# Matmuls on a zeroed tile ahead of the first product of a graph attention kernel

## What is computed

```
h = relu(layernorm(x));  x = x + smooth(h, adj)
h = relu(layernorm(x));  x = x + attention_and_mlp(h, adj, weights)

smooth:    B = (adj + adj.T) / 2 + I;  deg = sum(B, axis=1);  dinv = deg ** -0.5
           y = (adj @ (dinv[:, None] * B * dinv[None, :])) @ h
attention: 8 heads of 64, softmax over the neighbours, then four dense layers
```

## Time and profile before

| | |
|---|---|
| median of 3 runs | 863.55 us |
| all runs | 863.52, 863.55, 865.99 us |
| profiled execution: its own time | 865.98 us |
| its span (first to last instruction) | 864.2 us |
| TensorE matmul busy | 841.9 us, 97% |
| VectorE, ScalarE, GpSimd busy | 703.5, 427.9, 281.0 us |
| DMA | 87.97 MB, mean 102 GB/s |

### The profile page before, as it was taken

One profiled execution on the slowest core, in us unless ns is written; L12 is line 12 of the kernel. 1 busy time (PEld: TensorE's weight loads), 2 busy tenths in 40 slices (PEclk: granted clock), 3 DMA queues, 4 the chain that ended last, 5 costly groups with the idle time before them and its releaser, 6 DMA issues.

```text
span 864.2 us, 15276 instructions
## 1 busy us (share of the span) xinstructions
PE 841.9 (97%) x5207; PEld 757.4 (88%) x5207; DVE 703.5 (81%) x1224; ACT 427.9 (50%) x793; POOL 281.0 (33%) x299
## 2 busy tenths in 40 slices
PE   2999999999999999999999999999999999999998
PEld 2888888888888888887899999999999999999886
DVE  6899886557656885587999999999999999998864
ACT  3445333321111111256766666666666666785753
POOL 0000000000000000066875555555566644556322
PEclk9999999999999999999999999999999999999999
DMA  9979831703222222051340000000001022000144
GB/s 345 406 273 372 354 97 59 209 0 121 97 97 98 97 97 73 1 195 27 112 142 17 22 26 26 26 24 24 26 26 25 21 87 76 26 2 2 49 147 148
DMA packets 37627, 87.97 MB, mean 102 GB/s; under 512 B 7168, under 2 KB 8320, under 8 KB 37568
## 3 DMA queue, kind: packets, MB, share of 16 engines
q1 hardware_dynamic: 35504, 82.98, 27.7%
q10 hardware_dynamic: 2064, 4.26, 1.3%
HBM read 74.45 MB, written 12.78 MB: 101 GB/s over the span
## 4 chain that ended last, share of the span: by engine, by line
PE 92%; DMA 3%; DVE 3%; ACT 2%; issue 1%; POOL 0%; ACTq 0%
PE bank L1835 27%; PE bank L77 14%; PE bank L79 14%; PE bank L78 14%; PE bank L1879 14%; PE bank L554 3%; DMA l_src<-e_rows 1%; DMA e_rows<-rows 1%; PE bank L2413 1%; PE bank L2407 1%; PE bank L2352 1%; PE bank L2409 1%; DMA l_h<-x 1%; PE bank L1010 0%; DVE e L915 0%
## 5 line engine op out<-in xcount | busy, mean ns | idle before, releaser
L1359 DVE SCALAR_TENSOR_TENSOR l_q<-bank,neg_d,mask 128x512 fp32r<-128x512 f32 x512 | 339.0, 740 | 23.5 <-PE bank L1835 23.5
L1835 PE MATMUL bank<-l_parts,l_q 128*128 128x260 f32 x2048 | 250.5, 283 | 1.6 <-ACT l_o_m L1533 1.6
L1835 PEld LDWEIGHTS bank<-l_parts,l_q 128*128 128x128 f32 x2048 | 246.9, 188 | 2.6 <-ACT l_o_m L1533 1.9
L77 PE MATMUL bank<-x_hi,s_hi 128*128 128x512 f32 x448 | 174.5, 389 | 0.0
L79 PE MATMUL bank<-x_hi,s_lo 128*128 128x512 f32 x448 | 174.3, 389 | 0.0
L78 PE MATMUL bank<-x_lo,s_hi 128*128 128x512 f32 x448 | 174.3, 389 | 0.0
L784 POOL TENSOR_TENSOR l_prod<-wh,l_a 128x512 f32<-128x512 f32 x29 | 34.1, 1195 | 382.5 <-ACT wh L745 380.2
L1526 ACT ACTIVATE l_o_q<-bank 128x260 f32<-128x260 f32 x128 | 49.0, 388 | 104.7 <-PE bank L1835 97.5
L79 PEld LDWEIGHTS bank<-x_hi,s_lo 128*128 128x128 f32 x448 | 84.1, 188 | 17.6
L78 PEld LDWEIGHTS bank<-x_lo,s_hi 128*128 128x128 f32 x448 | 84.1, 188 | 17.3
L77 PEld LDWEIGHTS bank<-x_hi,s_hi 128*128 128x128 f32 x448 | 84.1, 188 | 17.3
(11 more groups left out here) (229 smaller groups left out, 1191.0 us busy)
## 6 DMA issues: line engine op xcount, KB each, us to landing
rows<-adj_t SPq DMA_DIRECT2D x48, 512.0 KB, 3.8
l_now<-adj SPq DMA_DIRECT2D x16, 512.0 KB, 7.0
l_rows_k<-adj_t SPq DMA_DIRECT2D x16, 512.0 KB, 7.9
l_src<-e_rows SPq DMA_DIRECT2D x32, 256.0 KB, 3.2
l_kept<-adj SPq DMA_DIRECT2D x12, 512.0 KB, 13.2
wh_store<-wh ACTq DMA_DIRECT2D x1, 4160.0 KB, 14.6
l_h<-x SPq DMA_DIRECT2D x4, 1024.0 KB, 17.2
x<-x SPq DMA_DIRECT2D x1, 4096.0 KB, 13.4
```

The costliest lines, as they stand in the source:

```text
L77: pe.matmul(acc, hi, rhs_hi, start=first, stop=False, skip_group_check=True)
L1359: v.scalar_tensor_tensor(out=q[:, i, :], in0=bank[S_BANKS[hh]][:], scalar=neg_d[:, i, h:h + 1], in1=mask[:, i, cols], op0=ALU.is_ge, op1=A ...
L1835: return pe.matmul(bank[Q_BANKS[hh][t]][:, 0:PW], q[:, i, t * P:(t + 1) * P], parts[pair_slot][:, i, hh * PW:(hh + 1) * PW], start=i == 0, ...
```

## The change

A third instruction on GpSimd zeroes the last 512 columns of `early_lo`, the place of the feature rests of step 3. TensorE waits for it and then multiplies that tile by itself: 36 matmuls of 128x128 by 128x512 into bank 7, then a wait for the first head of B (`hi_ready` 1), then 7 more. The results are dropped, since step 0 starts bank 7 anew. Everything behind it is as before.

```diff
@@ smooth_features
     def gpsimd(p):
         p.memset(ident[:], 0.0).then_inc(ident_made, 1)
         p.wait_ge(ident_made, 1)
         p.affine_select(out=ident[:], in_=ident[:], compare_op=ALU.not_equal, fill=1.0, base=0,
                         pattern=[[-1, P]], channel_multiplier=1).then_inc(ident_made, 1)
+        p.memset(early_lo[:, EARLY - 1, :].bitcast(F32), 0.0).then_inc(ident_made, 1)
     def tensor(pe):
+        def keep_busy(count):
+            for _ in range(count):
+                pe.matmul(bank[G8 - 1][:], early_lo[:, EARLY - 1, 0:P], early_lo[:, EARLY - 1, :], start=True, stop=True)
         pe.sem_inc(slot_free, 2)
+        pe.wait_ge(ident_made, 3)
+        keep_busy(36)
+        pe.wait_ge(hi_ready, 1)
+        keep_busy(7)
         def products(s, b, early=None, first=False, last=False, bank_free=None):
```

## The result

The changed kernel takes 867.27 us at the median of 14 runs (865.31 to 868.88), the kernel before 864.00 (863.1 to 865.99, 14 runs). The ratio is 1.0032, with a 95% interval of 1.0024 to 1.0040: 3.3 us slower by the medians, 2.8 (2.1 to 3.5) by the ratio, where 0.4 us less was forecast.

A forecast was written before the change was run, and what follows sets the result against it. TensorE, busy 97% of the span, was taken as the bound. Memset 0, filler 0, step 0 -2.98 and new idle time +2.58 sum to -0.40 us: 863.15 us from the median 863.55, range 861.8 to 865.7.

The forecast's parts named there:

- step 0: First 24 matmuls, from 15.50 us: at the upper clock they end at 20.94 instead of 23.92, 2.98 us earlier.
- steps 1 to 3: Following steps at the start: each waits for its feature head, cutting the gain to 1.99, 1.77 and 1.55 us.
- the chunk of x: Second chunk of x, landing near 41.5 us: decides when step 5 starts; nothing in the change makes it land sooner.
- step 5: Waits for the rest of B from `cut_lo(5)`: starts at 45.28 instead of 45.68, leaving only 0.40 us of gain.
- Past it the program is the same: Everything after the start: TensorE's waits are small and triggered loads start 0.40 us earlier too, so the gain persists.
- the filler at 0: Added matmuls from about 2.3 to 15.0 us, wholly in the 15.5 us wait before step 0: no cost.
- the row at 441.89: Wait of 1.65 us late in the kernel; matmuls behind it keep 0.120 us, so such a gap costs nothing.
- Rival 2: Slow stretch at the start is shorter in timed runs than profiled: no gain, 863.55; chance 0.22 together with another rival.
- Rival 4: Filler at the start runs late and delays step 0, so the kernel is slower: 866.5 us; chance 0.06.

The follow-up runs named there:

- g1: Kernel before plus 41 matmuls in a never-taken branch at the filler's place, no filler run: 866.75 us against 864.06, ratio 1.0025.
- e2: Changed kernel with the filler as two hardware loops of two 512-column matmuls per body: 864.50 us, ratio 1.0003 to the kernel before.
- e1: Changed kernel with the same 43 filler matmuls, of 16 columns instead of 512: 867.85 us, ratio 1.0041 to the kernel before.
- f4: Looped filler of e2 with the second chunk of x loaded ahead of tile 5: 863.38 us, ratio 0.9993 to the kernel before.
- g2: f4 run once more: 864.98 us, ratio 0.9998 to the kernel before.
- e3: Changed kernel with 128 filler matmuls of 16 columns instead of 43 of 512: 878.08 us against 863.97 for the kernel before.
- f2: Changed kernel with 26 + 7 filler matmuls and 92 more ahead in a never-taken branch: 864.84 us, ratio 1.0009 to the kernel before.
- f1: Changed kernel with 85 small matmuls added in the never-taken retry branch near the program's end: 866.12 us, ratio 1.0018 to the kernel before.
- f3: Kernel before with the second chunk of x loaded ahead of tile 5, no filler: 864.09 us against 864.15.
- e0: Kernel before, rerun unchanged: 865.02 us, with 863.97 for the same kernel beside it.

## Why the prediction was wrong

**What held.** The filler lay wholly in the wait (its last start is about 14.5) and raised the clock; step 0 lost nothing; VectorE and ScalarE held steps 1 to 3; the chunk of x held step 5. Of step 0's 2.98 us, 0.52 was left at step 5 (45.68 - 45.16), against 0.40. That this agrees so well is in part luck: beside the other four profiles without a raised clock (45.16 to 45.45), the changed kernel's 45.16 is 0 to 0.3 us sooner. On average the kernels with the filler and the old order of loads start step 5 at 45.04 (45.16, 45.01, 44.93, 45.05), the five without at 45.36. So some 0.3 us is the better figure for what the start gives.

**Where it failed.** The step is *"Past it the program is the same"*, and the sum in front of it, which had the filler at 0 because it ran in idle time. The filler's time was free, but its code was not: 43 matmuls with their weight loads are 86 instructions more in TensorE's stream, and everything behind them lies elsewhere in the 16 KB pieces in which that stream is fetched. A program with those instructions and without the filler's work (g1) is slower by 2.7 us, and one with the work and 16 instructions (e2) is not slower by anything that can be told. I never priced an instruction as an instruction. Two terms are missing:

- *The end, +1.6 us.* The over goes from 1.8 to 3.4. It does so with 86 instructions moved (changed, e1, g1), not with 16 (e2, f4, g2), nor with about 256 (e3, f2), and padding behind the middle of the program alone takes it back (f1). The closing events come 2.0 to 2.3 us after the last instruction in the three, 0.2 to 0.3 in all others. That the place of the code does this is shown. How it does so is not: the last fetch on record starts 0.0 to 0.5 us before the end of the span and ends 0.4 to 0.9 us behind it in all kernels alike, with the loss and without, and none is recorded after that. That the closing instructions lie beyond a border of a piece in the three, and so wait for it, is the reading that fits; the addresses themselves are not in the trace.
- *The store of scores, 5.55 to 6.71 us.* Its length has two values only: 5.53 to 5.62 in eight profiles and 6.71 to 6.73 in four, and the four are those whose code is moved by 86 in the middle. In these four a fetch of queue 8 starts 4.7 us after the store and lasts 0.9 us (between 432.2 and 434.0), and the store's last semaphore write follows 0.2 us behind the end of that fetch. In the eight others no fetch starts until 2.1 us or more after the store is complete. The packet is late by 0.6 us; the rest of the 1.16 us lies between its record and the end of the wait (0.9 us in the four, 0.3 in the others), and what fills it is not on record. In the profiles TensorE waits for the same chain anyway (1.65 us in the earlier trace rows), which hides some of it. In the timed runs the spans of g1 are 0.9 us longer at the median than before's beside them (863.2 against 862.3); as the end and this together make g1's 2.7 us, the difference gives 1.1.

**What is left.** 867.27 is 0.5 over g1, although the filler should have brought some 0.3 less, and e2, f2, f4 and g2, free of both losses, are not faster than before by what their starts gained. The start's gain is not lost early: in every profile TensorE's lead or lag against the kernel before is the same to 0.05 us at 395 us as at 60. What changes it comes behind 400 us. One part shows in the records. At the wait near 441 us the clock sometimes falls to its lower level. In e2's profile the wait is

```profile
439.94 7.31 PE L1845 MATMUL bank<-l_parts,l_q 128*128 128x260 f32 x45 [1.43 <-ACT l_o_m L1543]
```

and the stretches behind it (us, TensorE busy (x), granted clock, DMA share, GB/s) are

```profile
438.00:441.40 3.40, 1.96 (x13) 1.00 0.34 98
441.40:444.80 3.40, 3.40 (x18) 0.50 0.10 35
444.80:448.00 3.20, 3.20 (x29) 1.00 0.00 0
```

18 matmuls in 3.4 us where about 28 fit: the same 126 matmuls take 17.01 us here and 15.47 in the profile before, 1.5 us more. The prediction used the row at 441.89 to say that such a gap costs nothing; it costs nothing in some executions only. The profiles of f3 and g2 have the fall too, behind waits of 1.43 and 1.97 us, and those of the kernel before and e0 have none behind 1.65 and 1.71, so the length of the wait does not decide it.

The mean granted clock of each run tells how often it falls. Runs at 0.999 are hardly longer than those at 1.000; those at 0.998 or less have spans some 1.8 us longer (863.95 against 862.13 in the 81 runs of the kernel before). They are 30 of 70 in the kernels with a raised clock at the start and 31 of the 128 others, which makes 0.3 us on average. That is not the whole rest: among the runs at 0.999 or 1.000 alone, the mean span is 862.7 in e2 (9 runs) and 862.6 in f2 (5 runs), still 0.5 *over* the 862.1 of the kernel before. But e0, which is the kernel before itself, has 862.6 as well (9 runs), so half a microsecond between two sets of runs can be chance.

With the chunk of x ahead, the same mean is 861.5 (12 runs of f4 and g2), 0.6 under the kernel before, and at the lower values 863.3 against 863.95, again 0.6 under. So the two edits together may gain 0.6 us, which the more frequent fall (11 of 23 runs against 17 of 81) hides in the totals; sorted so after the fact, and with e0's scatter beside it, this is a hint and no proof. Why an early start should make the fall more frequent, and whether anything else costs e2 and f2 their gain, stays open.

**The rivals.** None was this one. Rival 2 came true in part: the slow stretch at the start of step 0 differs from run to run (the clock rises 4.5 to 6.1 us after the first matmul of the product in the six profiles where nothing had raised it), and the profile in hand had the longest. That takes away some of the gain and cannot make the kernel slower. Rival 4 had the sign and, by chance, nearly the size (866.5), but its mechanism, a late filler, did not occur. The range ended at 865.7, near the highest run of the kernel before, because every case in it took TensorE's start as the only thing that the change touched.

## What to carry to other kernels

Work put in idle time is free only if its code is: count the instructions that it adds, and where a 16 KB fetch then falls, at the program's end and beside the small DMAs that others wait for. Put filler in a hardware loop, where 44 matmuls cost 16 instructions here, and compare with a kernel that has the same instructions in a branch never taken; that tells code from work in one run. Compare a run's own time with its span before looking for a loss in the trace, since it may lie behind the last row.

## What the runs showed that I had not expected

- TensorE's stream is fetched through queue 8 in pieces of 16 KB that take 0.9 to 1.7 us each, 30 of them in the kernel before, and beside such a fetch the last 4-byte semaphore write of an unrelated store comes 0.6 us late.
- Matmuls on zeros raised the clock too: the filler's matmuls go at 0.427 us for the first nine and at 0.227 from 6.3 us on, after 4.3 us of them. 43 matmuls of 16 columns, at 0.213 us each, had not raised it; step 0 behind them was slow again.
- The slow stretch at the start is not in the granted clock, whose records begin with the rise (21.6 us in the kernel before, 6.3 in the changed one).
